# Attention with row maxima planned up to three units ahead, and index and selection joined in another way

## What is computed

```python
# causal attention: 16 heads, HD = 16, rotary part RD = 64, latents of 64
q, qr = heads(ql @ Wqu), rope(heads(ql @ Wqr));  k, v = heads(ckv @ Wku), heads(ckv @ Wvu);  kr = rope(x @ Wkr)
scores = (q . k + qr . kr) / sqrt(HD + RD);  masked causally;  out = softmax(scores) v Wo
# selecting attention: 16 index heads of 128, then 16 heads of 128 on the 32 best keys of each token
I = sum_h iw[t,h] * relu(qi[t,h] . ki[s]);  masked causally;  idx = top_k(I, 32)
p = softmax(q[t,h] . k[idx[t]] / sqrt(128));  out = (p v[idx[t]]) Wo
```

## Time and profile before

| | us |
|---|---|
| median of 3 runs | 2718.17 (2715.82 to 2718.72) |
| the profiled execution | 2713.48 |
| its span in the trace | 2711.7 |
| mean granted TensorE clock | 0.954 |
| PE busy | 2370.1 (87%) |
| weight loads (PEld) busy | 1832.4 (68%) |
| DVE busy | 1708.1 (63%) |
| ACT busy | 1342.0 (49%) |
| POOL busy | 1105.6 (41%) |

### The profile page before, as it was taken

How to read it: one execution, slowest core, us unless ns; L and a number is a source line. 1 busy time by engine, 2 the same in 40 slices (tenths; PEclk the granted TensorE clock), 3 DMA queues, 4 the chain that set the end, 5 groups by cost and what they waited for, 6 DMA issues and landing times. The chain is left out here.

```text
span 2711.7 us, 44725 instructions
## 1 busy us (share of the span) xinstructions
PE 2370.1 (87%) x15863; PEld 1832.4 (68%) x15863; DVE 1708.1 (63%) x3437; ACT 1342.0 (49%) x2719; POOL 1105.6 (41%) x997
## 2 busy tenths in 40 slices
PE   4976899899999994987989889889978999998799
PEld 4864555555555553776877777677767888777688
DVE  7547774766756826547555997979845545456343
ACT  3433446355454453343238876768655444344222
POOL 2552212102102101555316664636356567777232
PEclk9987999999999995998999999999989999999799
DMA  5233001000000004224000000000033233333200
GB/s 169 78 111 89 19 11 27 23 21 9 25 11 21 6 3 130 75 82 167 2 15 1 1 5 5 1 9 1 8 118 94 81 93 105 104 99 105 88 9 24
DMA packets 79653, 138.62 MB, mean 51 GB/s; under 512 B 27072, under 2 KB 48280, under 8 KB 78544
## 3 DMA queue, kind: packets, MB, share of 16 engines
q0 software_dynamic: 26512, 74.12, 9.1%
q1 hardware_dynamic: 52928, 61.64, 7.2%
HBM read 114.51 MB, written 20.94 MB: 50 GB/s over the span
## 5 line engine op out<-in xcount | busy, mean ns | idle before, releaser
L1501 ACT ACTIVATE PT<-ps 128x512 f32<-128x512 f32 (+3 forms) x640 | 298.6, 536 | 306.3 <-PE ps L1263 306.1
L2436 POOL DMA_INDIRECT KV<-kv_scratch,sidx x288 | 276.5, 960 | 131.7 <-issue 92.5
L35 PE MATMUL ps<-KIh,qih 128*128 128x512 f32 (+2 forms) x640 | 248.6, 388 | 51.7 <-DVE Isc L1936 41.4
L1379 DVE TENSOR_REDUCE xn<-ps 128x1 f32<-128x512 f32 x384 | 241.0, 682 | 35.7 <-PE ps L1248 33.4
L1996 POOL TENSOR_TENSOR part_sum<-part_sum,rlp 128x1024 f32<-128x1024 f32 (+7 forms) x120 | 210.6, 1755 | 88.1 <-ACT rlp L1831 87.1
L1936 DVE SCALAR_TENSOR_TENSOR Isc<-ps,iw,Isc 128x1024 f32<-128x1024 f32 (+7 forms) x216 | 208.7, 966 | 53.7 <-ACT ps L1855 48.6
L36 PE MATMUL ps<-KIl,qih 128*128 128x512 f32 (+2 forms) x640 | 240.0, 375 | 0.0
L37 PE MATMUL ps<-KIh,qil 128*128 128x512 f32 (+2 forms) x640 | 239.7, 375 | 0.0
L1855 ACT ACTIVATE ps<-ps,iwa 128x1024 f32<-128x1024 f32 (+7 forms) x240 | 198.2, 858 | 48.4 <-PE ps L37 48.0
L35 PEld LDWEIGHTS ps<-KIh,qih 128*128 128x128 f32 x640 | 125.0, 195 | 96.4 <-issue 75.3
L1246 PE MATMUL ps<-KH,QH 64*128 64x512 f32 (+2 forms) x640 | 136.1, 416 | 29.9 <-DVE xn L1379 13.3
(11 more groups left out here) (375 smaller groups left out, 6740.5 us busy)
## 6 DMA issues: line engine op xcount, KB each, us to landing
cs<-in_rope SPq DMA_DIRECT2D x20, 512.0 KB, 4.1
ycomb<-y_rows SPq DMA_DIRECT2D x16, 512.0 KB, 5.6
w1raw<-in_w SPq DMA_DIRECT2D x14, 512.0 KB, 6.8
KV<-kv_scratch,sidx POOLq DMA_INDIRECT x288
xn_rows<-xnr SPq DMA_DIRECT2D x8, 512.0 KB, 5.0
w2raw<-in_w SPq DMA_DIRECT2D x14, 256.0 KB, 7.3
wir<-in_wi SPq DMA_DIRECT2D x1, 2176.0 KB, 10.3
X<-in_x SPq DMA_DIRECT2D x1, 2048.0 KB
```

Source lines behind the costliest of these rows:

```text
L35: pe.matmul(out, lhs[0], rhs[0], start=start, stop=False)
L1379: v.tensor_reduce(part, o, AX_X, ALU.max).then_inc(a_free, 1)
L1501: s.activation(PT[:, rnd % 2, hh, lo:CH], ps[:, BANK[kind, u, j, r, hh % 2], lo:CH], ACT.Exp, scale=SCALE).then_inc(a_exp, 1)
L2436: g.indirect_dma_start(ring(k, m), None, a["kv_scratch"], bass.IndirectOffsetOnAxis(sidx[:, t % 2, at:at + 1], 0)).then_inc(rows_in[k % RB ...
```

## The change

In attention the mixing of one unit with the next is replaced. Query buffers are four deep (`QB`), KN exists twice (by the group's parity). A list `ahead` holds the preparation of units 1 to 15 in order, where each unit's first steps (weights, keys, queries) are put in front of the last three maxima steps of the unit before. Ahead of every step of `attend(u)` steps are taken from that list as long as they belong to a unit up to u + 3, are due (H 3.2 us after P, M 1.0 after H and 2.5 after the keys, R 0.6 after X, on the planner's clocks) and the planner's model of DVE's backlog is at most 1.5 us; what unit u + 1 still lacks is laid down at the end of unit u. The value projection leaves the stretch ahead of the loop: it becomes a step "V" for half the tokens of one group, 16 products of 128x64 into a ring bank, and ACT copies from there into VG; two such steps stand in `prepare(0)`, six in the c = 3 and c = 0 units, where copies stood before.

In the index the turning of the row numbers moves from the end to tiles 2 and 1, as one item ("named") in the ring of double banks. SP sends the first two pieces of the selection's weights after tile 4's last score product into room that the keys' columns no longer need, ACT casts them after tiles 2 and 1, and DVE makes the first piece's low part as the index's last operation. In the selection SP sends pieces 2 and 3 first of all, then the constants, and `swo` after the second low part; ACT casts pieces 2 and 3 ahead of the first pair's copy.

```diff
-        V = sb("V", [P, TILES, D], F32, a_ctx)
+        wv_h = sb("wv_h", [P, D], F32R, a_ctx)
+        wv_l = sb("wv_l", [P, D], F32R, a_ctx)
...
-        QH = sb("QH", [P, 2, NP, CH], F32R, a_ctx)
-        QLo = sb("QLo", [P, 2, NP, CH], F32R, a_ctx)
-        QN = sb("QN", [P, 2, NP, CH], F32R, a_ctx)
+        QB = 4
+        QH = sb("QH", [P, QB, NP, CH], F32R, a_ctx)
+        QLo = sb("QLo", [P, QB, NP, CH], F32R, a_ctx)
+        QN = sb("QN", [P, QB, NP, CH], F32R, a_ctx)
...
+        KN = [[XTh[:, 0, :], XTh[:, 1, :]], [XTl[:, 1, :], KN3[:]]]
...
-        PE_US = {"S": 0.96, "A": 1.1, "K": 0.94, "P": 1.41, "X": 0.0, "R": 0.2, "G": 1.5}
-        LAG_H, LAG_M, LAG_R, LEAD = 4.0, 1.6, 1.2, 5.0
+        PE_US = {"S": 0.96, "A": 0.88, "K": 0.94, "P": 1.41, "M": 0.47, "R": 0.2, "G": 1.5, "V": 1.8}
+        DVE_US = {"K": 1.45, "P": 2.0, "X": 0.35, "R": 0.3, "W": 0.7, "F": 0.7, "N": 0.7, "G": 1.4, "E": 0.25}
+        LAG_H, LAG_M, LAG_R, LAG_K, BACKLOG, RINGED, EARLY = 3.2, 1.0, 0.6, 2.5, 1.5, 2.2, 3
...
             if u % NCH == 0:
                 order = [("K", u, 0, 0)] + order + [("K", u, 1, 0)]
+                if u >= 1:
+                    order = [("W", u // NCH, p, 0) for p in range(NP)] + order
+                else:
+                    order += [("V", 0, half, 0) for half in range(2)]
...
-                    if j < NP:
-                        yield "W", g + 1, j, 0
                     if j == CT * 2 + 1:
                         yield "V", g + 1, 0, 0
...
+        def dve_us(step):
+            kind, u, h, r = step
+            if kind == "M":
+                return 1.26 if r[1][0] < u % NCH else 0.6 + 0.24 * (r[0] + 1)
+            return DVE_US.get(kind, 0.0)
 
         def steps():
             yield "O", 0, 0, 0
             yield from prepare(0)
+            ahead = []
+            for u in range(1, NU):
+                own = prepare(u)
+                first = own.index(("H", u, 0, 0))
+                at = [k for k, x in enumerate(ahead) if x[0] == "M" and x[1] == u - 1][-EARLY:]
+                at = at[0] if at else len(ahead)
+                ahead[at:at] = own[:first]
+                ahead += own[first:]
+            pe_at, dve_at, done, ended = 0.0, 0.0, 0, {}
+
+            def unit(x):
+                return NCH * x[1] if x[0] == "W" else x[1] + (x[0] == "K" and x[3] == 1)
+
+            def ready(x):
+                kind, u, h, r = x
+                if kind == "H":
+                    return ended["P", u, h, 0] + LAG_H
+                if kind == "M":
+                    keys = [("K", NCH * (u // NCH), h, half) for half in range(2)]
+                    return max([ended["H", u, h, 0] + LAG_M] + [ended[k] + LAG_K for k in keys if k in ended])
+                return ended["X", u, 0, 0] + LAG_R if kind == "R" else 0.0
+
+            def lay(x):
+                nonlocal pe_at, dve_at, done
+                pe_at = max(pe_at, ready(x), dve_at - RINGED if x[0] in "KPM" else 0.0) + pe_us(x)
+                if dve_us(x):
+                    dve_at = max(dve_at, pe_at) + dve_us(x)
+                ended[x] = dve_at if x[0] == "X" else pe_at
+                done += 1
+                return x
+
             for u in range(NU):
+                for step in attend(u):
+                    while done < len(ahead) and unit(ahead[done]) <= u + QB - 1:
+                        x = ahead[done]
+                        if ready(x) > pe_at or (dve_us(x) and dve_at > pe_at + BACKLOG):
+                            break
+                        yield lay(x)
+                    yield step
+                    pe_at += pe_us(step)
+                    if dve_us(step):
+                        dve_at = max(dve_at, pe_at) + dve_us(step)
+                while any(unit(x) <= u + 1 for x in ahead[done:]):
+                    yield lay(ahead[done])
...
-            for t in range(0, TILES, 2):
-                if t == 0:
-                    pe.wait_ge(a_pd, 3 * NCH)
-                else:
-                    pe.wait_ge(a_ve, max(t // 2 - 3, 0))
-                for m in range(2):
-                    tok = slice((t + m) * P, (t + m + 1) * P)
-                    o = ps[:, LAT_BANK + t // 2 % 4, m * D:(m + 1) * D]
-                    pe.matmul(o, CK[:, tok], wv_h[:], start=m == 0, stop=False)
-                    i = pe.matmul(o, CK[:, tok], wv_l[:], start=False, stop=m == 1)
-                i.then_inc(a_v, 1)
+            pe.wait_ge(a_pd, 3 * NCH)
...
+                elif kind == "V":
+                    o = take(kind, u, h, r, 0)
+                    for m in range(TILES // 2):
+                        tok = slice((TILES // 2 * h + m) * P, (TILES // 2 * h + m + 1) * P)
+                        heads = slice(GH * HD * u, GH * HD * (u + 1))
+                        pe.matmul(o[:, GH * HD * m:GH * HD * (m + 1)], CK[:, tok], wv_h[:, heads], start=m == 0, stop=False)
+                        i = pe.matmul(o[:, GH * HD * m:GH * HD * (m + 1)], CK[:, tok], wv_l[:, heads], start=False, stop=m == TILES // 2 - 1)
+                    i.then_inc(a_v, 1)
...
-                    before = NCH * u - 1
-                    s.wait_ge(a_av, ROUND[before, (TILES // 2 * (h + 1)) - 1] + 1)
-                    values(u, h)
+                    if u >= 1:
+                        s.wait_ge(a_av, ROUND[NCH * u - 1, (TILES // 2 * (h + 1)) - 1] + 1)
+                    s.wait_ge(a_v, 2 * u + h + 1)
+                    s.copy(VG[:, TILES // 2 * h:TILES // 2 * (h + 1), :, 0:HD],
+                           ps[:, BANK[kind, u, h, r, 0], :].rearrange("p (t h d) -> p t h d", h=GH, d=HD)).then_inc(a_vg, 1)
...
+            sp.wait_ge(i_L, SCORED[CT, NHI - 1, 0] + 1)
+            for m in range(2):
+                select_weights(sp, m, early[m][:])
...
+                    if t == NAMED_AT:
+                        key = ("named", 0, 0)
+                        room(key)
+                        pe.wait_ge(i_iw, SIGNED + 1)
+                        o = ibanks(key)
+                        for u in range(DENSE, TILES):
+                            for j in range(4):
+                                i = pe.matmul(o[TOPK * j:TOPK * (j + 1), TOPK * u:TOPK * (u + 1)], idxf[:, u, :], selt[:, j, :],
+                                              start=u == DENSE, stop=u == TILES - 1)
+                        i.then_inc(i_t, 1)
...
+            def selecting(m):
+                s.wait_ge(i_q, NCH * QP)
+                s.wait_ge(s_w[m], 16)
+                s.copy(swqh[:, w_piece(m)], early[m][:]).then_inc(s_wh, 1)
...
+                    if t in (2, 1):
+                        selecting(2 - t)
...
+                    if t == NAMED_AT + 1:
+                        v.wait_ge(i_k, SEARCHED[DENSE - 1])
+                        v.tensor_copy(idxf[:, DENSE:], idx[:, DENSE:]).then_inc(i_iw, 1)
+                    if t == NAMED_AT:
+                        v.wait_ge(i_t, NTB + 1)
+                        v.wait_ge(i_kvd[0], 16 * (TILES // 2))
+                        v.wait_ge(i_kvd[1], 16 * (TILES // 2))
+                        v.tensor_copy(idxT[:, DENSE:], ibanks(("named", 0, 0))[:, DENSE * TOPK:CH].rearrange("p (t g) -> p t g", g=TOPK)).then_inc(i_iw, 1)
...
-            v.tensor_copy(idxf[:, DENSE:], idx[:, DENSE:]).then_inc(i_k, 1)
-            v.wait_ge(i_t, NTB + 1)
-            v.wait_ge(i_kvd[0], 16 * (TILES // 2))
-            v.wait_ge(i_kvd[1], 16 * (TILES // 2))
-            v.tensor_copy(idxT[:, DENSE:], ps[:, 6, DENSE * TOPK:].rearrange("p (t g) -> p t g", g=TOPK))
+            v.wait_ge(s_wh, 1)
+            v.tensor_tensor(swql[:, w_piece(0)], early[0][:], swqh[:, w_piece(0)].bitcast(F32), ALU.subtract).then_inc(s_wl, 1)
...
-            weights(0)
+            for m in range(2, NW):
+                select_weights(sp, m, swr[:, m, :])
             sp.dma_start(sP[:, 0], first[:, :, 0:P]).then_inc(consts, 16)
             sp.dma_start(smk_raw[:, 0:P], a["smask"][:, 0:P]).then_inc(consts, 16)
             sp.dma_start(smk_raw[:, P:P + CH], a["smask"][:, P + CH:P + 2 * CH]).then_inc(consts, 16)
-            for m in range(1, NW):
-                weights(m)
             sp.dma_start(dV[:], first[:, :, P:2 * P]).then_inc(consts, 16)
-            sp.wait_ge(s_w[0], 16)
+            sp.wait_ge(s_wl, 2)
...
-            weights(0)
-            weights(1)
+            for m in range(2, NW):
+                weights(m)
...
-                if k in (1, 2):
-                    weights(k + 1)
...
-            masks(0)
-            for m in range(NW):
+            for m in range(1, NW):
+                if m == 2:
+                    masks(0)
                 v.wait_ge(s_wh, m + 1)
-                v.tensor_tensor(swql[:, w_piece(m)], swr[:, m, :], swqh[:, w_piece(m)].bitcast(F32), ALU.subtract).then_inc(s_wl, 1)
+                v.tensor_tensor(swql[:, w_piece(m)], early[1][:] if m == 1 else swr[:, m, :], swqh[:, w_piece(m)].bitcast(F32), ALU.subtract).then_inc(s_wl, 1)
```

(45 more changed lines are left out.)

77 lines of the change are left out of this document (30 added, 47 removed).

## The result

| | us |
|---|---|
| before, median of 4 | 2718.44 (2715.82 to 2719.80) |
| after, median of 4 | 2686.86 (2683.55 to 2693.61) |
| ratio | 0.9888, 95% interval 0.9865 to 0.9912 |
| profiled execution of after, span | 2690.06, 2688.3 |

The account below looks back on a forecast made before the run. PE was taken as the bound, idling for DVE's maxima in short units. Start -4, loop -29.9, index 0 and selection -6.5 sum to -40.4 from 2713.5, 2673.1; with 4.7 back, 2678 us, range 2655 to 2718.

Parts of the forecast that it names:

- Start, -4: Start of attention: with the value projection gone from ahead of the loop, keys start earlier; -4 us, bounds -2.5 to -5.
- Value steps, +9.6: Attention's loop: six value steps of 16 products at 0.10 us each lengthen PE's work; +9.6 us, ends +1.5 and +11.5.
- Look-ahead from unit 4 on, -36.5: Nine later short units of attention's loop lose idle time and half clock, keeping 7 us; -36.5 us, bounds -39.6 to -20.
- First group, -3, bounds 0 to -12: Units 0 to 2 of attention's loop: 12.6 us idle, no full unit ahead to take their maxima; -3 us.
- Index, 0: Index: its end gains 1.4 us, casts among tiles 2 and 1 take it back; 0 us, bounds -1 to +1.5.
- Selection, -6.5: Start of the selection: PE's first operands are ready at +0.3 instead of +6.3 us; -6.5 us, bounds -3 to -8.
- Held exponentials: Rival, attention's loop: ACT's query casts wait for POOL behind DVE's maxima, PE lacks exponentials; +17.2, 2735 us; chance 0.10.
- DVE as the pace: Rival, attention's loop: maxima run ahead only in dense runs, short units keep 5% idle; -21, 2697 us; chance 0.22.
- A look-ahead that moves nothing: Rival, attention's loop: the lists come out in nearly the old order; -0.9, 2717 us; chance 0.09.

Follow-up runs that it names:

- the old order: The changed kernel with attention's steps in exactly the order before the change; value steps, four query buffers, new index and selection stay: 2713.14 us, ratio 0.9979 to before.
- the joint alone: Only the index and selection parts of the change, on the attention of the kernel before: 2708.14 us, ratio 0.9975 to before.

## Why the prediction was right, and where it was not

*Start, -4.* Right. From the last latent product (243.18 before, 245.12 after) to the first score (271.56, 269.47) it took 28.4 us and now 24.4.

```profile
243.18 0.40 PE L37 MATMUL ps<-XTh,wp_l 128*128 128x512 f32 x1
```
```profile
245.12 0.40 PE L37 MATMUL ps<-XTh,wp_l 128*128 128x512 f32 x1
...
253.21 0.28 PE L1307 MATMUL ps<-wv_h,CK 128*128 128x64 f32 x1
253.32 0.28 PE L1308 MATMUL ps<-wv_l,CK 128*128 128x64 f32 x1
...
257.92 0.39 PE L1269 MATMUL ps<-KH,QH 64*128 64x256 f32 x2 [1.20 <-ACT QH L1513]
```

The way there was another: the value copies stood in front of the query's cast on ACT and held the first maxima at 257.92 (258.10 in the earlier trace rows).

*Value steps, +9.6.* The price per product was right, 0.11 us against the 0.10 taken from the earlier trace rows. The term was mis-sized all the same: the old order with the steps is only 5.2 us longer. A step in a full unit costs 1.6 to 1.7 us; what one costs in a short unit with gaps is not told apart from the clock. By the Trainium skill ("TensorE: Matmul & The Clock Gate", section "LDWEIGHTS (loading the stationary operand)") a load of 128 columns takes some 107 ns. The trace agrees: 64-column products start 0.11 us apart, as the 256-column ones of the earlier trace rows did (0.12), so it is not the columns that space the 64-column ones.

*Look-ahead from unit 4 on, -36.5.* Right in mechanism and a little small. The nine short units keep 7.4 us idle (7 forecast), and the clock is at 1.00. Against the old order units 4 to 15 lose 61.4 us, some 20 of them moved ahead.

*First group, -3, bounds 0 to -12.* This is the step that failed. I excluded a loss without a reason: I looked for units that could take work off units 0 to 2 and saw none, and did not ask what the new order does where nothing lies ahead. The kernel before shows the chain already, outside the rows that I read: over its loop PE waits 11.4 us, 12 times, for the joined maxima (L1389) and 5.0 for the DMA into QN. The old spread with its LEAD of 5 us was in the diff, and its removal in the first group is the cost: against the old order +33.8 us, 20 to 22 of it moved work by the estimate above, 11 to 13 lost at bare unit ends; PE's idle time alone grew by 11.4 (13.2 to 24.5). With the old spread back there the loop gains 38.0, near the forecast's 39.5 for both groups.

*Index, 0.* 608.1 after 609.8, a little beyond its bound of -1. *Selection, -6.5.* Right for the joint alone; in the profile of after it is missing, together with a stretch at half clock. I named the casts as what holds the pairs. They do in after, but with them out of the way smk's wait for the constants holds the same pairs, and the fifth pair's copy came to +11.6 only with both gone.

*Rivals.* By line within the loop of after (busy, mean ns | idle before, releasers), answering to the earlier trace rows:

```profile
L1269 PE MATMUL ps<-KH,QH 64*128 64x512 f32 (+2 forms) x624 | 130.7, 412 | 3.4 <-DVE xn L1410 1.4 <-DVE rb L1400 1.1 <-DVE xn L1414 0.8
...
L1513 ACT CAST QH<-rr 128x512 fp32r<-128x512 f32 x30 | 18.7, 624 | 0.0
```

Held exponentials: ACT's query casts still show no idle time ahead of them, and PE's waits for exponentials (PT) come to 1.6 us from unit 4 on, so nothing was held. DVE as the pace: out, PE idles 3.4 us ahead of the maxima's products where it idled 26.3. A look-ahead that moves nothing: the old order prices it at 0.9979, some 6 us faster than before (1 to 10), not the 0.9 forecast; the value steps cost 4 us less than their term.

With the measured terms (start, value steps, look-ahead with the first group's loss in it, joint) the sum is -4.0 + 5.2 - 27.6 - 6.8 = -33.2, beside 31.6 measured. That 2686.86 lies inside the range is in part luck: the first group's loss was excluded, and the value steps came out 4 us cheaper for a reason that the forecast didn't have.

## What to carry to other kernels

A planner that takes work ahead greedily needs a rule for the stretch where it has nothing ahead yet: end each chain of small steps (reduce, turn, DMA) some us of independent work before its result is needed, and look ahead only behind that. When work is moved between units, ask for each unit both who can take its work and what the new order leaves bare in it. And where an engine waits in order for two things in one place, taking the first away shows the second: read what is late next before pricing the gain.

## What the runs showed of the hardware

The granted clock fell behind gaps of 3 to 7 us on PE, in the first group down to a mean of 0.87 in a unit. Of six executions of the same selection code one ran at a clock of 0.68 from 10 to 15 us into the stage, and its last gather came at +523.1 us; the other five ran at 0.88 to 1.00 there and had it at +516.8 to +518.9. A low mean clock was not a cost of its own size: at 0.92 over the first group after lost 11 to 13 us, by estimate, and 11.4 us of that are added idle time of PE. Products without use ahead of the stage did not keep such a stretch out of it: with PE busy up to 1970 the clock fell to 0.52 from 1974 on, behind the next gap of 4.04 us.
